# A graph layer with experts: shorter edge records, later zero rows, and three smaller edits

## The reference

```python
xn = _layernorm(x)
x = x + gnn(xn, src, dst, edge_attr_20, edge_weight, edge_attr_3) + mix(xn)
x = x + moe(_layernorm(x))

# gnn: one row of x_ij per edge, summed per node idx_i = src
u = r_ij / norm(r_ij);  Yv = Y1_SCALE * u
h = softplus(f_ij @ Wf1 + bf1) - log 2
W = (h @ Wf2 + bf2) * rcut_ij[:, None]
m_s = s2(xs[idx_j], xv[idx_j], Yv) * W[:, :2 * F]
m_v = v2(xs[idx_j], xv[idx_j], Yv) * W[:, 2 * F:4 * F, None]
agg = segment_sum([m_s, m_v, ...], idx_i, num_segments=n)
S, V = agg_s @ W1_s, agg_v @ W1_v          # then softplus, W2_s, W2_v

# mix: linear attention, 8 heads of 64, then a layer norm with x + out
# moe: 8 experts, the best 2 per token, softmax of the two logits
y = silu(x @ w_gate[e]) * (x @ w_up[e]) @ w_down[e]
```

## Time and profile before

| what | value |
|---|---|
| median of 3 runs | 1680.25 us (1678.17 to 1683.88) |
| profiled execution, time | 1677.54 us |
| profiled execution, span | 1675.8 us |
| PE busy | 1448.5 us, 86% of the span |
| DVE, ACT, POOL busy | 852.4, 636.9, 759.3 us |
| mean granted TensorE clock | 0.927 |

### The profile page before, as it was taken

The page is one execution under the profiler, slowest core; times in us unless marked ns, Lnnn a source line. Parts: engine busy times, 40 slices in busy tenths (PEclk is TensorE's granted clock), DMA queues, the critical chain, the costliest instruction groups (busy, mean ns, idle before and its releaser), DMA issues. The chain is left out here.

```text
span 1675.8 us, 29431 instructions
## 1 busy us (share of the span) xinstructions
PE 1448.5 (86%) x8631; PEld 893.0 (53%) x8632; DVE 852.4 (51%) x1980; ACT 636.9 (38%) x1191; POOL 759.3 (45%) x783
## 2 busy tenths in 40 slices
PE   6466998777369999999999996678999999999995
PEld 3243454344124444444444443377787877887784
DVE  7745665577437777777777776452111111111111
ACT  2354555544226666666666664420100110000010
POOL 4577777777635655556565562006211111111111
PEclk7787999898679999999999998777999999999998
DMA  6665333332268888888888888531154252354113
GB/s 260 223 203 157 112 115 115 117 115 106 84 185 246 250 249 248 251 244 251 242 253 251 247 243 231 195 113 19 25 176 144 56 175 79 121 172 172 20 24 80
DMA packets 130911, 275.35 MB, mean 164 GB/s; under 512 B 21286, under 2 KB 68090, under 8 KB 129906
## 3 DMA queue, kind: packets, MB, share of 16 engines
q0 software_dynamic: 50432, 151.03, 30.5%
q1 hardware_dynamic: 80354, 121.25, 21.8%
q10 hardware_dynamic: 80, 2.56, 0.5%
HBM read 211.81 MB, written 65.50 MB: 165 GB/s over the span
## 5 line engine op out<-in xcount | busy, mean ns | idle before, releaser
L1048 POOL DMA_INDIRECT shared<-node_table,shared x343 | 324.2, 945 | 245.5 <-DVE msg L1116 144.6
L1608 PEld LDWEIGHTS psum<-zT,shared 128*128 128x128 f32 x2944 | 349.9, 193 | 66.6 <-issue 64.1
L1608 PE MATMUL psum<-zT,shared 128*128 128x128 f32 x2944 | 353.9, 276 | 9.1 <-issue 5.8
L394 POOL DMA_INDIRECT edge_list<-rec,place x313 | 311.4, 995 | 108.8 <-issue 94.7
L1118 DVE TENSOR_TENSOR msg<-shared,psum 128x768 f32<-128x768 f32 x339 | 321.2, 948 | 0.0
L1144 PE MATMUL psum<-wf,hT 128*128 128x512 f32 x678 | 315.3, 608 | 3.9 <-ACT psum L1080 3.9
L1080 ACT COPY psum<-bias 128x512 f32<-128x512 f32 x343 | 202.1, 590 | 194.6 <-DVE msg L1118 187.6
L1626 ACT ACTIVATE sg<-psum 128x128 f32<-128x128 f32 x184 | 51.0, 277 | 466.7 <-PE psum L1608 466.7
L1116 DVE TENSOR_TENSOR msg<-shared,psum 128x256 f32<-128x256 f32 x339 | 141.0, 416 | 148.9 <-PE psum L1144 147.4
L1672 DVE TENSOR_TENSOR hid<-sg,psum 128x128 f32<-128x128 f32 x184 | 52.6, 286 | 321.4 <-ACT sg L1626 321.4
L1144 PEld LDWEIGHTS psum<-wf,hT 128*128 128x128 f32 x678 | 122.3, 190 | 162.4 <-issue 144.0
(11 more groups left out here) (278 smaller groups left out, 1486.1 us busy)
## 6 DMA issues: line engine op xcount, KB each, us to landing
shared<-edge_list SPq DMA_DIRECT2D x356, 130.0 KB
shared<-in_L_ffn_w_gate SPq DMA_DIRECT2D x8, 2048.0 KB, 9.4
shared<-in_L_ffn_w_up SPq DMA_DIRECT2D x8, 2048.0 KB, 14.3
shared<-in_L_ffn_w_down SPq DMA_DIRECT2D x8, 2048.0 KB, 18.9
shared<-node_table,shared POOLq DMA_INDIRECT x343, 3.7
edge_list<-rec,place POOLq DMA_INDIRECT x313, 2.6
raw<-in_records SPq DMA_DIRECT2D x19, 256.0 KB, 3.5
xrow<-in_x SPq DMA_DIRECT2D x10, 250.0 KB
```

Source lines behind the costliest of these rows:

```text
L394: nc.gpsimd.indirect_dma_start(out=edge_list, out_offset=bass.IndirectOffsetOnAxis(ap=place[:n_, c:c + 1].bitcast(U32), axis=0), in_=rec[: ...
L1048: nc.gpsimd.indirect_dma_start(out=gat[:, k % G, :], out_offset=None, in_=table, in_offset=bass.IndirectOffsetOnAxis(ap=ix, axis=0)).then_ ...
L1608: ins = nc.tensor.matmul(GU[m % 2][:, o:o + BLK], w[u][:, j, m * P:(m + 1) * P], zT[:, j, :], start=(j == 0), stop=(j == DJ - 1))
```

## The change

1. **Records of 544 bytes.** RECW goes from 260 to 136: 128 hidden values, four factors (`RF`), the place within the group (`RAT`), the source index. DVE no longer makes `eq` in the front block but copies place and factors (two small copies per unit). In the edge block DVE makes the four one-hots of each tile, `hot`, by one instruction ahead of its two products, and PE takes them as weights.
2. **Zero rows later.** The five small zero DMAs stay ahead of the records, the three large ones (1.1 MB now) come after units 3, 5 and 7.
3. **Placing.** DVE parts six groups (group 4 first, into spare space `low`), POOL three. All offsets are read into registers ahead of the copies: 40 on ACT at the block's start, 24 on DVE between its subtractions and 12 after them. ACT also places the second half of group 0.
4. **First tokens.** `pick` and the token numbers are bfloat16, the number in two parts (its upper bits and its low five), so each product is one of two bfloat16 matmuls.
5. **Late gating.** ACT copies bank 4 to `yraw` and frees the bank; DVE scales `yraw` into `yo` at slice m = 5 of the next block (`gate`), after the loop for the last block. POOL waits for the new semaphore `gated`.

```diff
@@ -48,7 +48,7 @@
-RO, RDST, RECW = P, 2 * P, 2 * P + 4
+RF, RAT, RDST, RECW = P, P + 4, P + 5, P + 8
@@ -291,6 +291,7 @@
+            CLEAR_AT = {3 + 2 * d: d for d in range(ZG)}
@@ -378,10 +378,14 @@
-                    for d in range(ZI):
+                    def clear_rows(d):
...
+                    for d in range(ZG, ZI):
+                        clear_rows(d)
@@ -394,6 +398,8 @@
+                        if u in CLEAR_AT:
+                            clear_rows(CLEAR_AT[u])
@@ -727,12 +723,10 @@
-                        dve.wait_ge(eq_done, u + 1)
+                        nc.vector.tensor_copy(r[:, :, RAT], at_f[:, u * QC:u * QC + n_])
                         if u % FG == 0:
                             dve.wait_ge(cc_done, u // FG + 1)
-                        nc.vector.tensor_tensor(r[:, :, RO:RDST].rearrange("p j (v w) -> p j v w", v=4),
...
+                        nc.vector.tensor_copy(r[:, :, RF:RF + 4], cc[:, u // FG % 2, u % FG * QC:u % FG * QC + n_, :])
@@ -925,8 +919,6 @@
-                        if u < NQ:
-                            equal(u)
@@ -1113,6 +1106,9 @@
                             dve.wait_ge(summed, st + 1)
+                            r = er[:, k // TS, k % TS, :]
+                            nc.vector.scalar_tensor_tensor(hot[:, k % (2 * TS)], const[:, C_IOTA:C_IOTA + W].unsqueeze(1).to_broadcast([P, 4, W]), r[:, RAT:RAT + 1],
+                                                           r[:, RF:RF + 4].unsqueeze(2).to_broadcast([P, 4, W]), ALU.is_equal, ALU.mult)
@@ -1149,13 +1145,13 @@
-                                nc.tensor.matmul(SUMS[j * W:(j + 1) * W, 0:4 * P], er[:, u, j, RO:RO + W],
+                                nc.tensor.matmul(SUMS[j * W:(j + 1) * W, 0:4 * P], hot[:, (u % 2) * TS + j, 0, :],
@@ -1189,15 +1185,20 @@
+                def offsets(eng, groups):
+                    return {(g, j): eng.value_load(perm[0:1, g * TS + j:g * TS + j + 1], min_val=0, max_val=NB - 1) for g in groups for j in range(TS)}
@@ -1210,33 +1211,48 @@
-                    for g in reversed(range(1, NG)):
-                        nc.vector.tensor_tensor(agg[:, g, :], agg[:, g, :], agg[:, g - 1, :], ALU.subtract).then_inc(parted, 1)
+                    for g in (HALF_G, *reversed(range(HALF_G + 1, NG))):
+                        nc.vector.tensor_tensor(agg[:, g, :] if g > HALF_G else low, agg[:, g, :], agg[:, g - 1, :], ALU.subtract).then_inc(parted, 1)
+                        at.update(offsets(dve, (g,)))
...
+                @block.gpsimd
+                def _(pool):
+
+                    pool.wait_ge(parted, 1)
+                    for g in reversed(range(1, HALF_G)):
+                        nc.gpsimd.tensor_tensor(agg[:, g, :], agg[:, g, :], agg[:, g - 1, :], ALU.subtract).then_inc(parted_low, 1)
...
+                    at = offsets(act, reversed(range(NG)))
                     for i, g in enumerate(reversed(range(NG))):
                         act.wait_ge(agg_turned, i + 1)
-                        place_sums(act, nc.scalar.copy, i, g, 0, placed_a)
+                        place_sums(nc.scalar.copy, at, i, g, 0, placed_a)
+                    place_sums(nc.scalar.copy, at, NG - 1, 0, 1, placed_b)
@@ -1579,7 +1601,9 @@
-                            ins = nc.tensor.matmul(bank[5 + n_][:, 0:1], pick[:CR, n_, c, :], tok_f[:CR, c:c + 1], start=(c == 0), stop=(c == NC_ - 1))
+                            for k in range(2):
+                                ins = nc.tensor.matmul(bank[5 + n_][:, 0:1], pick[:CR, n_, c, :], tok_b[:CR, c, k:k + 1],
+                                                       start=(c == 0 and k == 0), stop=(c == NC_ - 1 and k == 1))
@@ -1620,10 +1644,15 @@
+                        act.wait_ge(y_mm, b + 1)
+                        act.wait_ge(gated, b + 1)
+                        nc.scalar.copy(yraw[:], bank[4][:]).then_inc(y_bank, 1)
@@ -1662,19 +1690,29 @@
+                    def gate(b):
+                        dve.wait_ge(y_bank, b + 2)
+                        dve.wait_ge(y_out, b * 16 + LISTED)
+                        dve.wait_ge(to_in, b * 16 + 16)
+                        nc.vector.tensor_scalar(yo[:], yraw[:], to[:, 1:2], None, ALU.mult).then_inc(gated, 1)
```

More of the change, by code:

```diff
@@ L1670, in _ @@
                                 copy_turned(b + 3)
+                            if m == GATE_AT and last is not None:
+                                gate(last)
                             dve.wait_ge(silu_done, b * HM + (m + 1))
                             nc.vector.tensor_tensor(hid[:, m, :], sg[:, m % 4, :], GU[m % 2][:, BLK:2 * BLK], ALU.mult).then_inc(hid_slots, 1)
-                        dve.wait_ge(y_mm, b + 1)
-                        dve.wait_ge(y_out, b * 16 + LISTED)
-                        dve.wait_ge(to_in, b * 16 + 16)
-                        nc.vector.tensor_scalar(yo[:], bank[4][:], to[:, 1:2], None, ALU.mult).then_inc(y_bank, 1)
+                    block_(0, None)
+                    with dve.Fori(1, nb) as b:
+                        block_(b, b - 1)
+                    gate(nb - 1)
 def _by_component(w):
```

62 lines of the change are left out of this document (32 added, 30 removed).

## The result

| what | before | after |
|---|---|---|
| median of 7 runs each | 1682.85 us | 1676.45 us (1674.39 to 1678.09) |
| ratio | 1 | 0.9962, 95% interval 0.9948 to 0.9977 |
| profiled execution, span | 1675.8 us | 1672.7 us |
| PE busy | 1448.5 us | 1451.1 us |
| DVE, ACT, POOL busy | 852.4, 636.9, 759.3 us | 880.9, 641.8, 763.2 us |

The change gains 0.38%. I had forecast 1665 us, and 1676.45 lies outside my range of 1656 to 1674. The two profiles show where the missing microseconds are. Each row is the length of one piece of the program between two instructions that exist in both kernels; the pieces add up to the difference of the spans.

The account below looks back on a forecast made before the run. It took POOL's queue to bound the front, PE the edge loop and experts, ACT's and DVE's placing the placing block. Terms summed to -14.9 us: 1677.5 to 1662.6 profiled, median 2.7 higher, so 1665 us, range 1656 to 1674.

Parts of the forecast that it names:

- Edge loop: Steady edge loop: `hot` lengthens DVE's step to 5.6 to 6.0 us, under PE's 6.36, so 0 us.
- decides from 0.38 us: Edge loop: DVE becomes the bound only from 0.38 us per `hot`; past the cover, 0.1 us per tile costs 34 us.
- The rival that named this loop: Edge loop: DVE becomes its bound, slower; at 0.50 us per `hot` it costs 40 us, 1705 us; chance 0.05.
- Front: Front block: 11.02 us gap goes, earlier start, late zeros cost 3.8 us; -9.3 us, between -12 and +2.
- allowance of 1.8 us: Front block: +1.8 us allowed for large zero DMAs lying ahead of records on the DMA engines.
- Start of the edge block: Wait for the second unit's records: half the bytes bring them about 1 us earlier; -1 us, 0 to -2.
- End of the edge block: POOL's wait and drain after the loop: half the record bytes end the wait earlier; -2 us, 0 to -5.
- Placing: Placing block: 40 reads at 0.54 us, then 44 copies taking 15 us; +1 us, from -6 to +4.
- Node, first tokens, gating: PE nearer the node block at high clock -0.5 us, earlier gather -1.4 us, PE's stall in expert block 1 gone -2.3 us.
- The end: End of the program: y goes through ACT (about 0.6 us) and then DVE; +0.6 us.
- The new copies: Front block rival: DVE's new copies lengthen POOL's scatters, 29 us if each holds one up, 1694 us; chance 0.02.
- The jam: Front block rival: zero rows and weights meet at units 5 to 8, POOL stands 8 to 11 us; 1674 us, chance 0.12.

Follow-up runs that it names:

- hot4_b: Changed kernel with a whole step's one-hots made together, ahead of DVE's wait for the filters and one step early, in three buffers: 1652.78 us, ratio to before 0.9815.
- dose_hot_b: Kernel before, long records kept, plus one DVE instruction of 128 elements per tile whose result nobody uses: 1708.27 us, ratio 1.0145.
- early_reads_c: Kernel of hot4_b with 32 of ACT's 40 offsets and all of DVE's 36 read at the start of the edge block: 1644.86 us, ratio to before 0.9773.
- zero_late_alone: Kernel before, records of 1040 bytes, with its three large zero DMAs after units 3, 5 and 7: 1672.68 us, ratio 0.9935.
- gate_early_c: Changed kernel with late gating undone, no copy on ACT, POOL waiting for `y_bank` again: 1681.14 us, ratio to before 0.9989.

## Why the prediction was wrong

1. *Edge loop, 0 us forecast, +24.8 measured.* This is the step that failed. I compared DVE's work per step, 5.6 to 6.0 us, with PE's 6.36 and called the rest cover; "four banks stand between DVE and PE" was meant to settle the rest. But DVE does its four tiles in one piece between two waits, and PE waits for the last of three seeds at once, which hangs on the last of these tiles. The path from PE's filters over DVE and ACT back to PE had 0.51 us of air per two steps, and four one-hots put 1.04 us on it. hot4_b (the same work off the path: 24.8 us back) and dose_hot_b (the instruction alone: a loop of 552.47 us against 552.53) show it. The rows that told it were beside the ones I read: DVE waits 1.49 us for PE in each step of before, and ACT's seed ends 6.66 us after the first filters. The instruction's cost was sized right (0.26 us per tile, within 0.20 to 0.285). The rule "decides from 0.38 us" was wrong: the loop pays from about 0.11. The price beyond it, "each 0.1 us per tile costs 84 x 0.4 = 34 us", was wrong the other way, since each turn of the ring spans two steps: from 0.11 to 0.26 us per tile the loop grew by 22.2 us (530.3 to 552.5), 15 us per 0.1. The rival that named this loop was right about the place and got 5%, with a price that began too late.
2. *Front, -9.3 forecast, -15.0 measured, and -3.2 at the joint.* The gap went, as said, and the start was 1.6 us earlier. The allowance of 1.8 us was not needed, and of the 3.8 us for the late zeros nothing is seen in the last scatter, since scatters got shorter (995 to 982 ns, 4 us; on the quick chips 995 to 1007 ns in four profiles with long records, 979 to 992 in six with short ones) and the stalls of 3 us went too. The drain that I "left" fell by 2.6 us. Three fronts of before end between 452.2 and 458.9 us and five of the changed kernel between 437.0 and 440.8: the profiled one of before was the quickest of its kind, which may be why the medians differ by 6.4 us and the profiles by 3.1.
3. *Start of the edge block, -1 forecast, +0.9.* Half the bytes brought the second unit no earlier. Over all profiles of the quick chips the first two steps take 25.1 to 26.9 us with either record.
4. *End of the edge block, -2 forecast, -2.2 measured,* but this is not shown: the same piece takes 10.3 to 11.6 us in four profiles with long records and 9.5 to 11.8 in six with short ones. If it was right, then by luck.
5. *Placing, +1 forecast, -1.3 measured.* ACT's first copy stands 21.57 us after the barrier, against 21.6 forecast. The copies took 12.9 us, not 15. The block's bound, the reads, was named rightly, and early_reads_c confirms it.
6. *Node, first tokens, gating: -4.2 forecast, -5.3 measured.* The node block takes 65.5 to 67.3 us in profiles of either kind. First tokens and gating are as forecast (-1.6; -2.2), and the last block's `to` did arrive in time.
7. *The end, +0.6 forecast, -1.9 measured.* The way over `yraw` costs 0.36 us, as forecast in kind (POOL's scatter-add starts 2.15 us after the last PE instruction, before 1.79). But the output's DMA behaves otherwise, see below.
8. *The other rivals.* The new copies did not lengthen scatters. The jam did not move: POOL waits nowhere more than 0.3 us after the first scatter. Taken without the loop, my sum was too cautious by 13 us.

## What to carry to other kernels

Before an instruction is added beside a full engine, compare it not with the free share of its own engine but with the air on the ring that it joins: follow the last buffer of a batch from its release to the instruction that waits for it, read how much later that instruction could start at no loss, and count how many steps the ring spans. Look also at whether the wait asks for more buffers than the next instruction needs. If the ring has less air than the instruction costs, make the instruction while the engine waits, from data that is there already, with one buffer more; here that turned a gain of 6 us into one of 30 (hot4_b). A busy engine's share can hide a lost 4%: count its instructions or measure the distance of like ones.

## What I had not expected of the hardware

- **POOL's drain** at the end of the front block took 7.992 us in each of six profiles with the large zero DMAs ahead of the records and 5.379 in each of the others, with them between, on quick and slow chips, though hundreds of scatters follow in both. I don't know what it waits for.
- **The output's DMA instruction** on ACT takes 2.40 us in before and 2.66 in zero_late_alone (2.38 to 2.71 in all kernels made from before), and 0.63 to 0.64 in every kernel made from the changed one, gate_early_c too, which has the old gating. It is 1.8 us shorter, about what the end of the span gained, and none of the five parts was seen to explain it. Before, then after:

```profile
1663.47 2.40 ACTq L1629 DMA_DIRECT2D out_x<-out_sums  x1
```

```profile
1662.53 0.63 ACTq L1658 DMA_DIRECT2D out_x<-out_sums  x1
```

- **Chips differ.** The same kernel before takes 1682 us on four chips and 1813 to 1827 on three, and a small gain can go with the chip: gate_early is level with before on a quick chip (ratio 0.9989) and 0.8 and 1.0% slower on two of the others. Each chip was met once, so whether it is the chip or its state at that time stays open.
